# A token-routing kernel on one core: ring places, level 1's first node at column 0, the fifth tile's constants ahead of the tree, and the last tiles normalised alone

## The reference, cut to what matters

```python
x = x + _L0_gnn_ref(xn, ...) + _L0_mix_ref(xn[None], ...)[0]
x = x + _L0_ffn_ref(_layernorm(x, axis=-1)[None], w1s, b1s, w2s, b2s)[0]

def _L0_ffn_ref(x, w1s, b1s, w2s, b2s):        # flat_x: 625 tokens of 256
    current = zeros(T)
    for _ in range(DEPTH + 1):                 # DEPTH = 7, 255 nodes
        all_nodes.append(current)
        score = einsum('td,td->t', flat_x, w1s[current]) + b1s[current]
        all_logits.append(score)
        current = current * 2 + (sign(score) + 1) / 2 + 1
    path_weights = gelu(abs(logits))
    for i in range(DEPTH + 1):                 # out += (x @ w2s[node] + b2s[node]) * weight
        t_i = einsum('td,tdo->to', flat_x, w2s[nodes_i]) + b2s[nodes_i]
        out = out + t_i * path_weights[:, i][:, None]
```

## Time and profile before

| | us |
|---|---|
| median of 3 runs | 336.35 (336.1 to 342.16) |
| the profiled execution | 337.33 |
| its span, first to last instruction | 335.6 |
| TensorE matmuls busy | 314.8 (94% of the span), 2685 instructions |
| VectorE busy | 236.7 (71%) |
| ScalarE busy | 162.3 (48%) |
| GpSimd busy | 127.8 (38%) |
| mean granted TensorE clock | 0.984 of full speed |
| bytes moved by DMA | 79.09 MB, mean 236 GB/s |

### The profile page before, as it was taken

One profiled execution on the slowest core, in us unless ns is written; L12 is line 12 of the kernel. 1 busy time (PEld: TensorE's weight loads), 2 busy tenths in 40 slices (PEclk: granted clock), 3 DMA queues, 4 the chain that ended last, 5 costly groups with the idle time before them and its releaser, 6 DMA issues. The chain is left out here.

```text
span 335.6 us, 9200 instructions
## 1 busy us (share of the span) xinstructions
PE 314.8 (94%) x2685; PEld 224.6 (67%) x2691; DVE 236.7 (71%) x689; ACT 162.3 (48%) x497; POOL 127.8 (38%) x249
## 2 busy tenths in 40 slices
PE   7998999999999999798999999999999999997980
PEld 2577869998878888484556666666666666663640
DVE  4846968974456546778889797889876677675680
ACT  2455756531171453374245655545556666653510
POOL 6400001003130314436006665665655555543565
PEclk9999999999999999899999999999999999999995
DMA  6991513737999400001649999999999999996015
GB/s 172 300 173 38 135 51 93 185 103 258 392 387 386 178 0 1 2 0 52 264 141 391 386 386 387 385 386 387 387 386 385 386 386 384 387 386 236 3 22 61
DMA packets 52611, 79.09 MB, mean 236 GB/s; under 512 B 3463, under 2 KB 20051, under 8 KB 52564
## 3 DMA queue, kind: packets, MB, share of 16 engines
q1 hardware_dynamic: 51154, 77.09, 66.2%
q0 software_dynamic: 720, 0.64, 1.7%
q10 hardware_dynamic: 690, 0.77, 0.8%
HBM read 77.21 MB, written 1.30 MB: 234 GB/s over the span
## 5 line engine op out<-in xcount | busy, mean ns | idle before, releaser
L1518 PE MATMUL ps<-reg,reg_w 128*64 (+1 forms) x688 | 154.9, 383 | 2.3 <-DMA reg<-in_L_ffn_w2s_dram 1.2
L1518 PE MATMUL ps<-reg,reg_m 128*64 128x256 f32 (+1 forms) x602 | 134.4, 380 | 0.0
L1518 PEld LDWEIGHTS ps<-reg,reg_w 128*64 128x64 f32 (+1 forms) x688 | 93.5, 138 | 53.3 <-issue 6.3
L655 POOL TENSOR_TENSOR reg_w<-reg_w 128x128 f32 x150 | 72.2, 482 | 79.5 <-ACT reg_w L922 68.4
L1518 PE MATMUL ps<-reg 125*67 125x22 f32 (+9 forms) x919 | 82.4, 245 | 1.4 <-DVE reg L1365 0.9
L1518 PEld LDWEIGHTS ps<-reg,reg_m 128*64 128x64 f32 (+1 forms) x602 | 81.0, 137 | 0.1
L1518 PEld LDWEIGHTS ps<-reg 125*67 125x67 f32 (+5 forms) x921 | 68.1, 127 | 13.8 <-issue 3.1
L921 ACT COPY reg_w<-ps 64x128 f32<-64x128 f32 x150 | 39.5, 263 | 58.4 <-PE ps L1518 58.4
L1457 DVE SCALAR_TENSOR_TENSOR reg_w<-reg_w,nid,reg 128x128 f32 x124 | 48.4, 393 | 22.1 <-PE ps L1518 18.9
L922 ACT COPY reg_w<-ps 64x128 f32<-64x128 f32 x150 | 39.3, 262 | 3.7
L1457 DVE SCALAR_TENSOR_TENSOR reg_m<-reg_w,reg 128x128 f32 x110 | 38.7, 352 | 0.2 <-issue 0.2
(11 more groups left out here) (276 smaller groups left out, 327.9 us busy)
## 6 DMA issues: line engine op xcount, KB each, us to landing
reg<-in_L_ffn_w2s_dram SPq DMA_DIRECT2D x127, 512.0 KB, 11.5
reg<-in_edge_attr_dram SPq DMA_DIRECT2D x13, 336.0 KB
reg<-in_L_gnn_Wc_dram SPq DMA_DIRECT2D x3, 512.0 KB, 5.8
reg<-in_L_gnn_Wn_dram SPq DMA_DIRECT2D x3, 256.0 KB, 4.8
out_dram<-acc SPq DMA_DIRECT2D x1, 512.0 KB
reg<-in_edge_attr_dram SPq DMA_DIRECT2D x13, 39.0 KB
reg<-in_L_mix_w_qkv_dram ACTq DMA_DIRECT2D x1, 384.0 KB, 4.7
reg<-in_x_dram ACTq DMA_DIRECT2D x2, 128.0 KB, 2.8
```

Source lines behind the costliest of these rows:

```text
L655: e.tensor_tensor(to, to, second[:, (BASE2[l] + k) % NSEC, :], ALU.add).then_inc(added, 1)
L1518: return e.matmul(to, lhsT, rhs, start=start, stop=stop, skip_group_check=True)
```

## The change

The region reg grows from 25,768 + 18,264 to 29,864 + 14,176 columns, and reg_q starts 4096 columns later; tiles that would have moved are given earlier places, so that most late ones keep theirs. EARLY, the pair from which the fetches wait for the stages ahead of the tree, goes from 25 to 29, and two waits of later pairs change their order. Level 1 gets ten steps of the moved path, in the order of its columns, the first with node 0 and a constant place in the ring, and its fixed path has node 1 alone. The constants of the fifth tile are made by one pair of full products into bank 7 ahead of the tree, copied by ScalarE and added by GpSimd; the list B2_AT loses its last two entries, and the whole of acc is stored after step (4, 12). In the last layer, tiles 3 and 4 are normalised one by one, the shift of the fifth tile stands behind the statistics of the first three, and the tokens of these stand ahead of the fourth tile's sum.

```diff
-EARLY = 25
+EARLY = 29
...
+FIXED = {l: [n for n in range(2 ** l) if n < HEAD or n % 2] if l != END else [1] for l in SORTED}
+MOVED = {l: 2 ** l - len(FIXED[l]) if l != END else 0 for l in SORTED}
+UNITS = {l: MOVED[l] + NW - (l != END) for l in SORTED}
...
-B2_AT = ((6, 36), (3, 8), (2, 4), (2, 5), (2, 6), (2, 7), (2, 8), (4, 12), (7, 68), (5, 20))
+B2_AT = ((6, 36), (3, 8), (2, 4), (2, 5), (2, 6), (2, 7), (2, 8), (4, 12))
...
                 if p == EARLY + 5:
+                    e.wait_ge(p_sort, 4)
+                    e.wait_ge(p_tok, 1)
+                if p == EARLY + 8:
                     e.wait_ge(colp_ready, 1)
                     e.wait_ge(s_gwT, NT)
-                if p == EARLY + 7:
-                    e.wait_ge(p_sort, 4)
-                    e.wait_ge(p_tok, 1)
...
+            e.wait_ge(added, UP[B2_AT[-1]] + 1)
             e.dma_start(out[0:4 * TP, :].rearrange("(t p) d -> p t d", p=TP), acc[:, 0:NT - 1, :]).then_inc(s_acc, 16)
+            e.dma_start(out[4 * TP:4 * TP + 112, :], acc[0:112, NT - 1, :]).then_inc(s_acc, 16)
             e.dma_start(out[4 * TP + 112:N, :], acc[112:LAST, NT - 1, :]).then_inc(s_acc, 16)
...
@@ GpSimd, ahead of its tree loop @@
+            e.wait_ge(s_gwT, NT + 1)
+            c(e.tensor_tensor(acc[:, NT - 1, :], acc[:, NT - 1, :], consts, ALU.add))
             e.wait_ge(tabs_u, TABS["addresses"])
...
@@ ScalarE, in the last layer after the copy of w1T, and among the x_T copies @@
+                        e.wait_ge(l_r, NL * NT + 1)
+                        e.activation(rstd[:, 0:NT - 2], rv[:, 1, 0:NT - 2], ACT.Sqrt).then_inc(l_sq, 1)
...
             x_T(1)
+            e.wait_ge(l_r, NL * NT + 2)
+            e.activation(rstd[:, NT - 2:NT - 1], rv[:, 1, NT - 2:NT - 1], ACT.Sqrt).then_inc(l_sq, 1)
             x_T(2)
             x_T(3)
+            e.wait_ge(l_r, NL * NT + 3)
+            e.activation(rstd[:, NT - 1:NT], rv[:, 1, NT - 1:NT], ACT.Sqrt).then_inc(l_sq, 1)
...
@@ ScalarE, after the copies to gwT @@
+            e.wait_ge(p_gwT, NT + 1)
+            e.copy(consts, ps[:, 7, 0:D]).then_inc(s_gwT, 1)
...
@@ VectorE, the order at the end of the last layer @@
             tile_sum(NT - 3)
-            last_shift(NT - 1)
             tile_stats(NT - 3)
             norm_stats(0, NT - 2)
+            last_shift(NT - 1)
+            norm_tokens(0, NT - 2)
             tile_sum(NT - 2)
-            norm_tokens(0, NT - 2)
             tile_stats(NT - 2)
+            norm_stats(NT - 2, NT - 1)
             tile_sum(NT - 1)
+            norm_tokens(NT - 2, NT - 1)
             tile_stats(NT - 1)
-            norm_stats(NT - 2, NT)
-            norm_tokens(NT - 2, NT)
+            norm_stats(NT - 1, NT)
+            norm_tokens(NT - 1, NT)
...
@@ VectorE, tree and outputs @@
-                e.wait_ge(used, BASE[END] + 2 * j + 1)
+                e.wait_ge(used, BASE[END] + 2 * j + 2)
                 e.wait_ge(added, len(UPPER))
...
+                    masked(lhs[:, u % NLHS, :, :], t,
+                           k * WIN if l == END else within(offs[u % RU] & 1023, (NW - 1) * WIN),
+                           0.0 if (l, k) == (END, 0) else nid[:, u:u + 1]).then_inc(lhs_full, 1)
...
-                    if l == END and k == 7:
+                    if l == END and k == 6:
                         tile_out(0)
...
@@ TensorE @@
-            keep_busy(7, 10)
+            keep_busy(7, 13)
...
             logits(2)
+            logits(3)
             x_T(4)
-            logits(3)
             logits(4)
...
-            keep_busy(0, 2)
             e.wait_ge(s_sort, 4)
             e.wait_ge(s_gwT, 4)
             e.wait_ge(s_tok, 1)
             for b in range(5):
                 mm(ps[:, b, :], zeros_b[:, 0:128], zeros_b[:, :], True, True)
-            keep_busy(4, 3)
+            e.wait_ge(s_gwT, NT)
+            for h in range(2):
+                ins = mm(ps[:, 7, 0:D], gwT[0:128 - h, h, (NT - 1) * TP:R], b2t[0:128 - h, h, :], h == 0, h == 1)
+            ins.then_inc(p_gwT, 1)
+            keep_busy(4, 1)
...
                     if k == 1 and t < len(ORDER) - 1:
+                        if t == 0:
+                            e.wait_ge(s_gwT, NT + 1)
                         spread(t + 1, 0)
...
+                    at_w = k * D if l == END else within(at[u % RU] & 4095, (NW - 1) * D)
+                    if (l, k) == (END, 0):
+                        at_n = 2 * PAIR0[END] % RING * 2 * D
```

More of the change, by code:

```diff
@@ L58 @@
 PLACE = {l: t for t, l in enumerate(ORDER)}
-FIXED = {l: [n for n in range(2 ** l) if n < HEAD or n % 2] for l in SORTED}
-MOVED = {l: 2 ** l - len(FIXED[l]) for l in SORTED}
-UNITS = {l: MOVED[l] + NW - 1 for l in SORTED}
+FIXED = {l: [n for n in range(2 ** l) if n < HEAD or n % 2] if l != END else [1] for l in SORTED}
+MOVED = {l: 2 ** l - len(FIXED[l]) if l != END else 0 for l in SORTED}
+UNITS = {l: MOVED[l] + NW - (l != END) for l in SORTED}
 BASE = {l: sum(UNITS[m] for m in ORDER[:PLACE[l]]) for l in SORTED}
@@ L139, in part16 @@
             return flat.rearrange(f"p ({' '.join(names)}) -> p {' '.join(names)}", **dict(zip(names, dims)))
-        reg = sb("reg", [128, 25768 + 18264])
-        xin = part(reg, 25768 + 12824, 128, NT, D)
+        reg = sb("reg", [128, 29864 + 14176])
+        xin = part(reg, 29864 + 12824, 128, NT, D)
         acc = sb("acc", [128, NT, D])
         vecT = sb("vecT", [128, 2, 13])
-        vec_b = part(reg, 25768 + 11800, 128, 4 * D)
+        vec_b = part(reg, 29864 + 11800, 128, 4 * D)
         gamma_b, beta_b, bout_b, gout_b = (vec_b[:, v * D:(v + 1) * D] for v in range(4))
@@ L205, in graph_layer @@
         reg_r = reg[:, 0:25768]
-        reg_q = reg[:, 25768:]
+        reg_q = reg[:, 29864:]
         reg_m = sb("reg_m", [128, 1280])
@@ L228, in graph_layer @@
         dhot = part(reg, 11124 + HR * EG * JX, EP, HR * EG * 2, WX)
-        raw = part(reg, 25768 + 5376, EP, ED, EG * 2 * DE)
+        raw = part(reg, 29864 + 5376, EP, ED, EG * 2 * DE)
         wn = part(reg_r, 17040, 128, 2, NL, D)
@@ L281, in graph_layer @@
         side = part16(reg_q, 5120, 128, BF16, NT, 256, 2)
-        onpath = part(reg_q, 5720, 128, NT, 256)
-        xp = part16(reg_q, 7000, 128, BF16, 3, NT, D)
-        Pm = part16(reg_q, 8920, 128, BF16, NT, R)
+        onpath = part(reg_q, 9000, 128, NT, 256)
+        xp = part16(reg_q, 7080, 128, BF16, 3, NT, D)
+        Pm = part16(reg_q, 5480, 128, BF16, NT, R)
         Gw = part(reg_w, 4420, NW - 1, LEAVES)
@@ L289, in graph_layer @@
         starts = part16(reg_q, 5160, 128, BF16, R)
-        sel = part16(reg_q, 17752, 3 * LEVELS, BF16, LEVELS, 128)
-        first = part(reg_q, 16472, 1, U)
-        gwT = part(reg_q, 15192, 128, 2, R)
+        sel = part16(reg_q, 13656, 3 * LEVELS, BF16, LEVELS, 128)
+        first = part(reg_q, 13300, 1, U)
+        gwT = part(reg_q, 11096, 128, 2, R)
         xsT = part(reg_w, 1280, 128, 2, R)
@@ L303, in graph_layer @@
         nrow = reg_w[:, 0:2 * R].bitcast(I32)
-        xs = [part(reg_q, 16472, 128, 2, R), part(consts_sb, 0, 128, 2, R)]
+        xs = [part(reg_q, 12376, 128, 2, R), part(consts_sb, 0, 128, 2, R)]
         lhs = part(reg_w, 4672, 128, NLHS, 2, WIN)
@@ L519, in _ @@
                 pair(p)
-            e.wait_ge(added, UP[B2_AT[2 * NT - 3]] + 1)
+            e.wait_ge(added, UP[B2_AT[-1]] + 1)
             e.dma_start(out[0:4 * TP, :].rearrange("(t p) d -> p t d", p=TP), acc[:, 0:NT - 1, :]).then_inc(s_acc, 16)
[L524 to L527, removed]
+            e.dma_start(out[4 * TP:4 * TP + 112, :], acc[0:112, NT - 1, :]).then_inc(s_acc, 16)
             e.dma_start(out[4 * TP + 112:N, :], acc[112:LAST, NT - 1, :]).then_inc(s_acc, 16)
-            e.wait_ge(s_acc, 64)
+            e.wait_ge(s_acc, 48)
             e.wait_ge(s_out, 16 * NT)
@@ L564, in _ @@
             for l in SORTED:
-                ins = e.iota(kk[:, COLS[l]], [[2, UNITS[l]]], base=HEAD, channel_multiplier=0,
+                ins = e.iota(kk[:, COLS[l]], [[2, UNITS[l]]], base=HEAD - 2 * (l == END), channel_multiplier=0,
                              allow_small_or_imprecise_dtypes=True)
@@ L855, in cut @@
                 e.copy(xp[:, q, i0:i1, :], frm[:, i0:i1, :]).then_inc(x_cut, 1)
-            e.wait_ge(l_r, NL * NT + 1)
-            e.activation(rstd[:, 0:NT - 2], rv[:, 1, 0:NT - 2], ACT.Sqrt).then_inc(l_sq, 1)
             def x_T(i):
@@ L1307, in norm_tokens @@
             def norm_tokens(i0, i1):
-                e.wait_ge(l_sq, NL * NT + (1 if i0 == 0 else 2))
+                e.wait_ge(l_sq, NL * NT + 1 + max(0, i0 - NT + 3))
                 for i in range(i0, i1):
@@ L1390, in _ @@
                 c(e.tensor_reduce(out=Ow[:, l:l + 1], in_=Gw[:, ::LEAVES >> l], axis=AX.X, op=ALU.add))
-                s, n = LEAVES >> l, min(HEAD, 2 ** l)
-                c(e.tensor_scalar(tab_v[:, BASE[l]:BASE[l] + n], pre_i[:, 0:n * s:s], 960, 10,
+                s, n, n0 = LEAVES >> l, min(HEAD, len(FIXED[l])), FIXED[l][0]
```

(1 more changed line is left out.)

5 lines of the change are left out of this document (removed).

## The result

| | before | after |
|---|---|---|
| median, 21 runs each | 336.61 us | 334.03 us |
| lowest and highest | 335.48 to 342.16 | 333.03 to 338.50 |
| ratio, 95% interval | | 0.9914 (0.9897 to 0.993) |

The changed kernel is 0.9% faster, about 2.9 us by the ratio, which is taken over the undisturbed runs alone; the medians differ by 2.6. The forecast was 330.8 us, and the range 328.4 to 333.4 misses the median by 0.6 us.

A forecast was written before the change was run, and what follows sets the result against it. Bounds: late ring transfers stalling TensorE in the tree, an all-engine chain before it, GpSimd's scatters after. 3.0 + 1.8 + 0 + 0.8 = 5.6 us off 337.33 gave 331.7; off the median, 330.8 us, range 328.4 to 333.4.

The forecast's parts named there:

- the tail: Level 1 to the end: earlier tile 0 outputs bring the last scatter 0.8 us forward, ends 0 and 1.4.
- the second scatter: End of kernel: three masked operands on VectorE delay tile 1, so it starts at 321.9; GpSimd alone would allow 321.3.
- the step from the profiled execution to the median: Final sum: the runs' median 336.35 is 1.0 us below the profiled 337.33, so 331.7 becomes 330.8.
- the front: Last layer's norm ahead of the tree: 1.8 us gained, ends -0.5 and 2.2.
- the last token: Last layer's norm: the fifth tile's token is ready at 143.1 against 144.1, 1.0 us earlier.
- the logits: Behind the last token: VectorE's 0.81 us wait for the fourth tile's logits goes, 0.8 us gained.
- front worth little: Rival: the clock falls again later or another chain holds; some 0.4 of 1.8 us stay, 332.2 us, chance 0.17.
- the ring: Tree: four more early pairs and earlier waits remove TensorE's transfer stalls, 3.0 us gained, ends 0 and 3.0.
- the constants at no cost: Fifth tile's constants ahead of the tree: GpSimd's extra sum of about 0.75 us costs 0, ends 0 and 0.5.
- the two SBUF sides: First scatter: VectorE's two-input masked operands could hold up GpSimd, making the sum 331.2 in place of 330.8.
- the ring runs dry: Rival in the tree: queue emptied before pair 40; loss of 1 to 3 us, 332.8 on average, chance 0.13.
- slower: Rival: the ring's late pairs transfer more slowly; 341.4 us if a piece takes 10% longer, chance 0.03.

The follow-up runs named there:

- pad8: The changed kernel with eight tiny unused memsets added early on GpSimd; 331.72 us, ratio 0.9859 to the kernel before.
- ring_only: The kernel before with only the new reg layout, EARLY at 29 and SyncE's two moved waits; 334.47 us, ratio 0.992.
- after_again: The changed kernel as it is, run and profiled once more; 334.13 us, ratio 0.9928 to the kernel before.
- before_pad122: The kernel before with 122 memsets added on GpSimd; 337.02 us, ratio 1.000.
- norm_only: The kernel before with only the statistics' order, split square root, thirteen dummies and logits(3) ahead of x_T(4); 336.30 us, ratio 0.998.
- pad40: The changed kernel with forty memsets added early on GpSimd; 331.76 us, ratio 0.9866 to the kernel before.
- tail_only: The kernel before with only the part on level 1 and the fifth tile's constants; 338.83 us, ratio 1.0037.
- before_pad125: The kernel before with 125 memsets added on GpSimd; 337.18 us, ratio 1.0004.

## Why the prediction was wrong

**Wrong: the tail.** The step that failed reads "First scatter 1.06 us later, as now (322.6 to 323.64)", behind tile 0's outputs. It was 3.19 us. What lies ahead of it came nearly as forecast: one sum of GpSimd ahead of the outputs, and outputs that end 3.75 us behind the 158th step (316.98 - 313.23) where they ended 4.82 behind it (322.59 - 317.77), 1.07 us earlier (1.4 forecast). The forecast of 0.8 us for the last stretch is met, and passed, where the fetch lies elsewhere: 17.82 became 16.69 in pad8, -1.1. There a second error shows, which cost nothing: the prediction let the masked operands hold back the second scatter, to 2.64 us behind the first (321.9 - 319.26), but in pad8 it starts 2.07 us behind (320.14 - 318.07), as in before. With the fetch the last stretch was 18.90, +1.1, outside the term's own ends of 0 and 1.4 us of gain. The trace of before had the sign: its own packet stands at 320.81, during GpSimd's last sum and just ahead of the 1.3 us in which it waits for tile 0 anyway (321.26 to 322.59). The prediction treated the distance from outputs to scatter as a constant of the hardware, but it was the constant of one instruction count. The term missed by 1.9 us.

**Wrong: the step from the profiled execution to the median.** The prediction took 1.0 us off because the profiled execution was that much above the median. But what set it apart was the fall of the clock near 140, worth 1.3 us, and the front's 1.8 us had that gain in it already. It was counted twice: 1.0 us. A fall, wherever it lies, shows in the mean clock of a run: of the 78 runs of before beside the experiments 41 had 0.986 or less, and of the 39 runs of the kernels that have the norm's part 9. Without such a fall, before stands at 336.0 and the changed kernel at 333.8 beside it (eight and six runs above 0.986), 2.2 us, which is 0.27 + 3.2 less 1.1 within 0.2.

**Right in kind, a little large: the front.** 1.57 us came of 1.8, and 1.3 of them are the clock. The prediction had it as 1.0 for the last token and 0.8 for the logits. Against a run of before without the fall the last token isn't earlier at all (142.32 + 0.74 - 134.44 = 8.6 us behind the anchor in ring_only, 9.0 in after_again): the split's extra operations cost what they had been bounded by. What is gained comes from the comparisons, which wait 0.90 us in ring_only and not at all in after_again. They leave VectorE 0.5 us ahead (its next row starts at 147.17 - 134.45 = 12.72 behind the anchor, then at 146.75 - 134.55 = 12.20). The products behind them take 2.92 us in place of 2.67, and 0.27 is left at the tree; why they take longer was not looked into. The rival "front worth little" gave it 0.4 for the wrong reason (the clock falls again); its size is right for executions of before whose clock did not fall near 140.

**Right: the ring.** 3.0 us forecast, 3.2 measured in the changed kernel and in ring_only; 3.4 to 3.5 against before_pad122 and norm_only, whose trees took 143.8 and 143.7 us. Pair 40 landed 3.8 us after its issue (forecast 3.6), pair 86 5.9 (forecast 4.7). No later pair came short, so the rivals "the ring runs dry" and "slower" did not occur.

**Right: the constants at no cost.** GpSimd's sum took 1.03 us where 0.75 were forecast, and its first tree sum came at 174.72, yet TensorE never waited: the front is 38.43 with the part and 38.42 without.

**Not borne out: the two SBUF sides.** The rule of the Trainium skill (SBUF — State Buffer, "SBUF: two separate sides") was weighed as possibly holding up the first scatter by a masked operand. No run tests it on the scatter itself, since the masked operands are over when it starts: in pad8 they run from 317.05 to 317.93 and the scatter from 318.07. What the runs show is that they don't delay its start, 1.05 us behind the outputs in pad8 as in before. And the 0.23 us by which the first scatter is longer than the others are not theirs: it takes 1.77 us in after_again as well, where it starts at 320.17, 2.2 us behind their end.

The miss in sum: 1.9 for the fetch, 1.0 counted twice, 0.2 for the front, and 0.2 that passed ahead of it, less 0.2 for the ring: 3.1 of the 3.2 us between 330.8 and 334.0.

**The better kernel.** The change with three to forty memsets on GpSimd took 331.7 to 331.8 us in each of its three forms (ten runs in all), 1.3 to 1.7% below before, and is the fastest of this study.

## What to carry to other kernels

Look where the packets of the instruction queue lie before an edit that adds or takes instructions on GpSimd: in a wait they are free, between the last wait and a scatter that everything waits for they cost 2.1 us. A few instructions that do nothing move the edge, and any later edit can move it back, so it has to be looked at again each time. And when a profiled execution stands above the median, find what sets it apart before taking the difference off: a term of the sum may hold it already.

## What the runs showed of the hardware

- GpSimd's program comes in pieces of 8192 bytes, one for each 128 instructions (the packets of pad40), and the place of their edges repeats with 128 instructions: no memset and 128 memsets gave the same 3.19 us from the outputs to the first scatter, three, eight and forty gave 1.05.
- Such a piece costs 2.1 us when it is asked for behind the last wait and ahead of the first scatter (2.4 in tail_only), at most 0.3 us when it falls among the sums (pad8), and nothing that can be seen when it falls under a wait (before, before_pad125) or behind the first scatter's start (before_pad122). The packet itself moves in 0.3 to 0.6 us. In the late cases it starts 1.05 to 1.06 us behind the start of GpSimd's last recorded instruction (1.34 in tail_only), and the next one starts 1.77 us behind the packet's start; what fills the rest the profile does not show. That GpSimd asks for it some instructions ahead of the edge would fit the narrow place, but was not shown.
- TensorE's clock fell to 0.50 (1.2 GHz) for 3.4 us near 140 after an idle gap of 1.7 us in some executions, and in others of the same gap it stayed at 1.00 (2.4 GHz). One fall cost 1.3 us here. With the gap at 0.27 us it fell there in none of seven profiles.
